# Perceiver block on one Trainium2 core: VectorE's fills, mask and layer-norm variances placed elsewhere in the query stage

## What is computed

```
x = x + _L0_xattn_ref(_layernorm(x, axis=-1), ctx_1024, _lenS2, Wq, Wk, Wv, Wo, q_norm_w, k_norm_w)
    # _layernorm: m = mean(x); v = var(x); (x - m) / sqrt(v + 1e-05)
    # _L0_xattn_ref: qh = rms_norm((q @ Wq) per head, q_norm_w); kh = rms_norm((kv @ Wk) per head, k_norm_w)
    #                mask = arange(s) < x_seqlens;  attn = softmax(where(mask, qh kh^T / 8, -1e9));  o = (attn vh) @ Wo
x = x + _L0_attn_ref(_layernorm(x), ...)
x = x + _L0_ffn_ref(_layernorm(x), ...)
```

## Time and profile before

| | us |
|---|---|
| median of 3 runs | 2426.11 |
| lowest, highest | 2424.57, 2427.75 |
| the profiled execution | 2425.77 |
| its span in the trace | 2423.9 |
| PE busy | 2319.3 (96%) |
| DVE busy | 2101.4 (87%) |
| ACT busy | 1363.6 (56%) |
| POOL busy | 1485.0 (61%) |

### The profile page before, as it was taken

One profiled execution on the slowest core, in us unless ns is written; L12 is line 12 of the kernel. 1 busy time (PEld: TensorE's weight loads), 2 busy tenths in 40 slices (PEclk: granted clock), 3 DMA queues, 4 the chain that ended last, 5 costly groups with the idle time before them and its releaser, 6 DMA issues. The chain is left out here.

```text
span 2423.9 us, 57393 instructions
## 1 busy us (share of the span) xinstructions
PE 2319.3 (96%) x16343; PEld 1961.3 (81%) x16343; DVE 2101.4 (87%) x3379; ACT 1363.6 (56%) x2591; POOL 1485.0 (61%) x1069
## 2 busy tenths in 40 slices
PE   6888999999999999999999999999999999899985
PEld 3666888888888888888888888888888888788743
DVE  6779999999999999999999999999999997558776
ACT  4744555555555555555555555555555554355646
POOL 3446777777777777777777777777777772001100
PEclk9999999999999999999999999999999999999987
DMA  2432222222222222222222222222222214331000
GB/s 92 158 125 48 47 56 54 54 54 54 54 54 54 54 54 54 54 53 53 53 54 54 55 59 55 54 53 53 53 53 53 53 46 136 124 106 37 2 1 18
DMA packets 441099, 145.04 MB, mean 60 GB/s; under 512 B 365344, under 2 KB 423616, under 8 KB 440896
## 3 DMA queue, kind: packets, MB, share of 16 engines
q1 hardware_dynamic: 440880, 143.50, 23.9%
q10 hardware_dynamic: 144, 0.52, 0.1%
HBM read 109.17 MB, written 34.73 MB: 59 GB/s over the span
## 5 line engine op out<-in xcount | busy, mean ns | idle before, releaser
L456 POOL TENSOR_TENSOR probs<-arena,best_all 128x1024 f32 (+2 forms) x397 | 943.2, 2376 | 422.0 <-DVE best L835 401.3
L1079 PEld LDWEIGHTS u_ps<-rows,probs 128*128 128x128 f32 x6656 | 801.3, 192 | 56.7 <-issue 13.7
L1079 PE MATMUL u_ps<-rows,probs 128*128 (+1 forms) x6656 | 812.5, 276 | 9.8 <-ACT probs L661 5.0
L820 DVE SCALAR_TENSOR_TENSOR arena<-s_ps,mask,rrms 128x512 f32 (+2 forms) x832 | 603.6, 727 | 113.4 <-PE s_ps L956 112.2
L661 ACT ACTIVATE probs<-probs 128x1024 f32<-128x1024 f32 (+1 forms) x416 | 440.9, 1061 | 418.9 <-POOL probs L456 404.1
L795 DVE TENSOR_REDUCE ssq<-squares 128x16 f32<-128x1024 f32 (+2 forms) x416 | 490.3, 1179 | 37.2 <-ACT squares L619 36.0
L619 ACT ACTIVATE squares<-k_ps 128x512 f32<-128x512 f32 (+1 forms) x832 | 450.6, 590 | 41.6 <-PE k_ps L956 21.9
L835 DVE TENSOR_TENSOR best<-best,arena 128x1024 f32<-128x1024 f32 (+1 forms) x352 | 448.3, 1274 | 0.1
L954 PE MATMUL k_ps<-w_hi,cT_hi 128*128 128x512 f32 (+1 forms) x832 | 362.4, 436 | 4.4 <-ACT squares L619 4.4
L613 ACT ACTIVATE cT_hi<-cT 128x128 fp32r<-128x128 f32 (+1 forms) x416 | 129.2, 311 | 365.5 <-DVE cT L786 365.4
L954 PE MATMUL s_ps<-q_hi,cT_hi 128*128 (+2 forms) x832 | 330.4, 397 | 3.1 <-DVE arena L820 3.0
(11 more groups left out here) (245 smaller groups left out, 2209.7 us busy)
## 6 DMA issues: line engine op xcount, KB each, us to landing
stage<-in_ctx SPq DMA_DIRECT2D x1536, 16.0 KB, 1.7
rows<-in_ctx SPq DMA_DIRECT2D x32, 768.0 KB
queries<-probs SPq DMA_DIRECT2D x16, 1024.0 KB, 4.0
q_plain<-queries SPq DMA_DIRECT2D x32, 512.0 KB, 3.4
best_all<-best_rows SPq DMA_DIRECT2D x31, 512.0 KB, 3.7
u_transposed<-uT_sb SPq DMA_DIRECT2D x124, 128.0 KB, 2.6
a_uT<-u_transposed SPq DMA_DIRECT2D x10, 1024.0 KB, 4.9
arena<-u_transposed SPq DMA_DIRECT2D x6, 1024.0 KB, 4.9
```

The lines of the kernel that those rows point to most:

```text
L456: pool.tensor_tensor(probs[0:r, slot_of(c, PRING), :], scores_at(b, c), best_all[0:r, bass.ds((b % 2) * HL, HL)], ALU.subtract).then_inc(s ...
L820: dve.scalar_tensor_tensor(out=scores_at(p, c, h * HALF, HALF).rearrange("p (h l) -> p h l", l=L), in0=s_ps[h][0:r, :].rearrange("p (h l) ...
L1079: last = pe.matmul(u_ps[g // 3][:, at:at + UW], probs[0:r, s, g * P:(g + 1) * P], rows, start=(c == 0 and g % 3 == 0), stop=(c == NC - 1), ...
```

## The change

DVE's list is written in another order, and `layernorm_variance` is cut into four parts (mean; centred rows; squares; variance), each with its own waits on one semaphore, `ln_var`, which now counts six for a chunk. The work itself is the same, instruction for instruction.

- The 26 fills and the fill of `ssq` stand in front of everything on DVE, ahead of `layernorm_variance(0)`.
- `make_mask` and `layernorm_variance(1)` stand behind `layernorm_scale(0)`, ahead of step 0.
- `w_lo` stands in step 2 instead of step 0.
- The four parts of `layernorm_variance(2)` stand at the ends of steps 0 to 3, those of `layernorm_variance(3)` at the ends of steps 4 to 7, each ahead of the step's `layernorm_scale` and `turn`.

```diff
@@ ACT: rough_layernorm(j)
-                act.wait_ge(ln_var, 2 * j + 2)
+                act.wait_ge(ln_var, 6 * j + 6)
@@ DVE: layernorm_variance
-            def layernorm_variance(j):
+            def layernorm_variance(j, quarter):
...
+                if quarter == 0:
+                    dve.wait_ge(x_in[j], 16)
+                    dve.tensor_reduce(stat[:, 0, :], x3, AX_X, ALU.add).then_inc(ln_var, 1)
+                    dve.wait_ge(ln_var, 6 * j + 1)
+                    dve.tensor_scalar(stat[:, 1, :], stat[:, 0, :], 1.0 / D, None, ALU.mult).then_inc(ln_var, 1)
+                elif quarter == 1:
+                    dve.wait_ge(ln_var, 6 * j + 2)
+                    dve.tensor_tensor(xn3, x3, bc(stat[:, 1, :], [P, CHUNK, D]), ALU.subtract).then_inc(ln_var, 1)
+                elif quarter == 2:
+                    dve.wait_ge(ln_var, 6 * j + 3)
+                    dve.tensor_tensor(xsq3, xn3, xn3, ALU.mult).then_inc(ln_var, 1)
+                else:
+                    dve.wait_ge(ln_var, 6 * j + 4)
+                    dve.tensor_reduce(stat[:, 2, :], xsq3, AX_X, ALU.add).then_inc(ln_var, 1)
+                    dve.wait_ge(ln_var, 6 * j + 5)
+                    dve.tensor_scalar(stat[:, 3, :], stat[:, 2, :], 1.0 / D, EPS, ALU.mult, ALU.add).then_inc(ln_var, 1)
@@ DVE: query(i)
-                if i == 0:
-                    for j in range(2 * NC):
-                        dve.memset(rows1[:, j * UW + D:j * UW + D + 1], 1.0).then_inc(ones_ready, 1)
-                    dve.memset(ssq[:, :], 0.0).then_inc(ssq_clear, 1)
-                    dve.wait_ge(ssq_clear, 1)
-                    make_mask()
-                    layernorm_variance(1)
+                if i == 2:
                     dve.wait_ge(w_hi_ready, 1)
                     dve.tensor_tensor(w_lo[:, :], u_sb[:, :], w_hi[:, :], ALU.subtract).then_inc(w_ready, 1)
-                if i % CHUNK == 0 and CHUNK <= i < TILES - CHUNK:
-                    layernorm_variance(i // CHUNK + 1)
+                if i + 2 * CHUNK < TILES:
+                    layernorm_variance(i // CHUNK + 2, i % CHUNK)
                 if i % CHUNK == 1 and i + 3 < TILES:
                     layernorm_scale((i + 3) // CHUNK)
@@ DVE: ahead of the steps
-            layernorm_variance(0)
+            for j in range(2 * NC):
+                dve.memset(rows1[:, j * UW + D:j * UW + D + 1], 1.0).then_inc(ones_ready, 1)
+            dve.memset(ssq[:, :], 0.0).then_inc(ssq_clear, 1)
+            dve.wait_ge(ssq_clear, 1)
+            for quarter in range(4):
+                layernorm_variance(0, quarter)
...
             layernorm_scale(0)
+            make_mask()
+            for quarter in range(4):
+                layernorm_variance(1, quarter)
             each_step(dve, query, step)
```

More of the change, by code:

```diff
@@ L719, in layernorm_scale @@
                 dve.wait_ge(ln_rough, j + 1)
-                newton(dve, stat[:, 3, :], stat[:, 4, :], stat[:, 5, :], stat[:, 0, :], ln_steps, 7 * j + 4)
-                dve.wait_ge(ln_steps, 7 * j + 7)
+                newton(dve, stat[:, 3, :], stat[:, 4, :], stat[:, 5, :], stat[:, 0, :], ln_steps, 3 * j)
+                dve.wait_ge(ln_steps, 3 * j + 3)
                 dve.tensor_tensor(xn3, xn3, bc(stat[:, 0, :], [P, CHUNK, D]), ALU.mult).then_inc(xn_ready, 1)
```

## The result

| | before, us | after, us |
|---|---|---|
| median | 2426.74 (4 runs) | 2411.67 (4 runs) |
| lowest, highest | 2424.57, 2427.75 | 2408.80, 2413.31 |
| the profiled execution, its span | 2425.77, 2423.9 | 2413.20, 2411.4 |

The ratio is 0.9938, with a 95% interval of 0.9921 to 0.9955: 15.1 us between the medians, and 12.6 us between the two profiled executions. Predicted was 2410.6, 1.1 us under the median, in a range from 2406 to 2418.5.

A forecast was written before the change was run, and what follows sets the result against it. PE's some 33 us idle in the query stage, behind ACT's waits for DVE's variances, was taken as the bound; 6.8 + 3.2 + 6.8 - 1.3 = 15.5 us off the median 2426.11 gave 2410.6 us, range 2406 to 2418.5.

The forecast's parts named there:

- Fills: Fills at DVE's front, before x lands at 3.94: cost 0, allowed 0 to 0.3 us.
- Mask and `layernorm_variance(1)` in the gap: In DVE's idle time before save_q(0): done by 14.5, PE delivers at 14.69, 0.2 us to spare; 0 to 0.5 allowed.
- Term A: Steps 0 to 3: ACT's 4.71 us wait goes and save_q comes earlier; gain 6.8 us, between 5.5 and 7.3.
- that chain keeps its lengths: Steps 1 to 3: POOL's L475 still starts 2.94 us after save_q and ends 1.90 later, setting the next save_q.
- the first rival, clock: PE stays at 1.2 GHz longer in tiles 2 and 3: gain 12, 2414 us; chance 0.20 shared with DVE-bound steps.
- Term B: Step 4: one whole variance leaves, the step falls from 9.10 to 5.91 us; gain 3.2, between 2.3 and 3.2.
- Term C: Steps 8 and 9: the other variance leaves, 13.1 us instead of 19.93; gain 6.8, or 5.9 if steps cost 7.0.
- Term D: Steps 5 to 7: the variance parts cost time as DVE and POOL block each other; -1.3 us, between 0 and -3.8.
- The sum: All four terms together: 6.8 + 3.2 + 6.8 - 1.3 = 15.5 us gained.
- Everything behind it is the same length.: After the query stage: later passes keep their length, so the stage's gain of about 15.5 us comes out whole.

The follow-up runs named there:

- sp_later: The changed kernel with SP's context loads one query step later, so query stores stand ahead of them: 2411.77 us, ratio 0.9941.
- wlo_3: The changed kernel with w_lo in step 3 instead of step 2: 2408.29 us, ratio 0.9927.
- before_again: The kernel before the change, unchanged, run for a second trace: 2428.41 us (one run).
- after_again: The changed kernel, unchanged, run again beside its variants: 2411.98 us, ratio 0.9952.
- wlo_1: The changed kernel with w_lo in step 1 instead of step 2: 2410.02 us, ratio 0.9934.
- parts_only: The changed kernel with fills, mask, layernorm_variance(1) and w_lo back behind save_q(0), variances still in parts: 2417.45 us, ratio 0.9967.
- best: The changed kernel with w_lo in step 1, SP's context loads one step later and filler matmuls in PE's idle time: 2410.26 us, ratio 0.9932.
- early_w: The changed kernel with w_hi ahead of step 0, w_lo in DVE's front gap, mask in step 17, SP's loads one step later: 2410.85 us, ratio 0.9953.

## Why the prediction was right, point by point

**What bounds the kernel.** Right for the stage: PE's busy time there stayed, its idle time went. That what is won comes out whole at the end is not what the profiled execution shows: 13.5 us at the last save, 12.5 at the end, with 8.7 in the passes between.

**Fills.** 0, as predicted: 1.84 to 2.85, with 1.26 us to spare before x lands.

**Mask and `layernorm_variance(1)` in the gap.** Right, but the 0.2 us to spare were 0: the lengths landed 0.3 us later (10.24 instead of 9.95), and the end is a dead heat at 14.6.

**Term A, predicted 6.8.** It is 6.13 us at full clock (`sp_later`, 38.44 - 32.31) and 4.88 in after. `save_q` of steps 1 to 3 was put at 17.45, 22.3 and 27.15 and stands at 17.34, 22.47 and 27.77. The step that failed is "that chain keeps its lengths". POOL's small instruction behind `save_q(2)` took 0.75 us instead of 0.21, since DVE's `w_lo` and squares stand there. POOL's timeline of after:

```profile
24.20 0.75 POOL L463 TENSOR_TENSOR arena<-arena 128x16 f32<-128x16 f32 x1 [1.68 <-ACT arena L560]
...
25.92 1.90 POOL L475 TENSOR_TENSOR arena<-arena 128x1024 f32<-128x1024 f32 x1
```

L475 ends at 27.82 instead of 27.2, and both PE's turn and DVE's L734 wait for it: 0.6 of the 0.7 us. `wlo_3` bears this out: with `w_lo` gone from there the small one takes 0.22 us, and PE's turn starts at 27.48 instead of 28.01 in `sp_later`. The other 1.25 us in after are the first rival, clock: it was set against a sentence that "no gap over 2 us is left there", and one of 2.54 us is left. It cost 1.3 us and not 3.7, because only the turn and one half ran slow.

**Term B, 3.2.** 9.10 less 5.91 is 3.19. That it is exact is in part luck of the trace: in `before_again` the same step takes 10.26 us, as PE runs at half clock behind the 3.11 us of idle time, and the term is 4.35.

**Term C, 6.8.** 19.93 less 14.12 is 5.8 in after, and 19.93 less 13.14 is 6.8 in `sp_later`. The wait for the store (0.68 us, and 0.2 in the next step) is most of the difference. The prediction spoke of SP only for the context loads; a shorter step brings the need for a buffer forward, and where SP's loads are issued slowly the store behind them doesn't move with it. The 6.8 us also hold something that the prediction did not see. In before, `save_q(9)` starts as PE's L974 ends, and that took 2.05 us at half clock instead of 1.12. By an estimate from these two numbers, 0.9 of the 6.8 us are the clock, which came back because the 3.64 us of idle time went.

**Term D, -1.3.** Steps 5 to 8 take 18.10 us against 17.74: -0.36. The price of the lock was mis-sized because DVE came first. DVE and POOL in step 5 of after:

```profile
42.38 0.69 DVE L726 TENSOR_TENSOR arena<-arena 128x512 f32<-128x512 f32 x1
...
44.24 0.93 DVE L734 TENSOR_SCALAR arena<-arena 128x16 f32<-128x16 f32 x1
```

```profile
42.61 0.54 POOL L469 TENSOR_TENSOR arena<-arena 128x16 f32<-128x16 f32 x1
43.23 1.90 POOL L475 TENSOR_TENSOR arena<-arena 128x1024 f32<-128x1024 f32 x1
```

L726 runs in 0.69 us, where the price was taken from one that took 2.39, and POOL's small one is stretched instead, to 0.54. The Trainium skill (SBUF — State Buffer, section SBUF: two separate sides) has whoever starts first hold the shared ports for the whole instruction; these rows agree, on both sides: 0.93 us for 0.17 on DVE, 0.54 for 0.22 on POOL.

**The sum, 15.5.** At full clock and without the store's wait it is 6.13 + 3.19 - 0.36 + 6.79 = 15.8 us (`sp_later`). In after's trace it is 4.88 + 3.19 - 0.36 + 5.81 = 13.5. Both are against the first trace of before; against the second, after's gain at the last save is 15.9. So the stage gives 13.5 to 15.9 us, and the forecast of 15.5 is right in its mechanism. That the median's 15.1 us comes within 0.4 of it is partly luck: in the profiled execution the stage gave 2 us less than the sum, 4.8 were lost behind it (4.3 of them in the two places shown), and 3.8 won at the end. Other executions have other sums, and no trace shows that of the median. The other 0.6 of the 1.1 us by which the forecast was off is before's own median, 2426.74 us here and 2426.11 when the sum was made.

**"Everything behind it is the same length."** Wrong in the profiled execution by 4.8 us one way and 3.8 the other. A gain as in the clock rival (12) is what it had, 12.6, though of the places that the rival named only the turn and half of step 4 ran slow.

**The clock rival's evidence.** It was set against the reading that after the 3.11 us of the earlier trace rows PE "ran on at full rate". That holds for the one trace; in `before_again` it did not, and in before itself it did not behind the 3.64 us of step 9.

## What to carry to other kernels

Work that stands behind a wait of another engine can be moved into idle time ahead of it, and the gain can be read step by step from the spacing of one repeated instruction; add for each moved two-input DVE instruction what the large and also the small POOL instructions beside it do, and for each shortened step which buffer is needed earlier and what its store is queued behind. Where a gain of some 15 us is to be refined by 1 us, compare traces at a marker inside the stage, since the time of the whole carries the clock of all later stages. Take such a marker from two traces of the same kernel before a single difference is believed. And when a wait is removed, look whether PE ran slow behind it: part of the gain may be its clock.

## What the runs showed of the hardware

**The clock after short idle times is not the same from one execution to the next.** Behind the same 2.54 us of PE idle time the turn ran in 1.94 us in both traces of after and in 1.06 in `sp_later`. Behind the 2.2 us ahead of the first product with the values, the 16 matmuls took 2.02 us in both traces of before, in `after_again` and in `wlo_1`, and 2.93 to 3.67 us in the other seven traces without fillers. In `wlo_1` it fell behind 1.40 us of idle time, in after (126.25) behind 0.88, and in `parts_only` behind 0.79: the group of 16 at 123.82 took 1.90 us for 1.16. The Trainium skill (TensorE: Matmul & The Clock Gate, section HAM oscillation — how this bites in real kernels) puts the fall of the clock down to long idle gaps between groups of matmuls; in these traces it also fell at gaps of 0.79 to 2.54 us, so short ones aren't safe. What decides it in an execution was not settled.

**The mean clock goes with the spread.** The runs of one kernel lie 1.3 us (`best`) to 8.7 us (`early_w`) apart, and the slowest have a lower mean granted clock than the fastest: 2406.39 us at 0.991 and 2413.85 at 0.988 for `wlo_1`. By an estimate from these, a mean of 0.001 less over 2410 us is 2.4 us of work at full clock. That this clock causes the difference, and isn't caused by it, was not tested apart.

**A column of 16 is enough to be stopped.** DVE's L734, 128x16 with one input, takes 0.17 us where it comes before POOL's L475 (25.15 in `wlo_3`) and 1.81 behind it (26.04 in after). DVE's 128x1024 sum, L731, wasn't lengthened: it ran from 19.79 to 21.00 in after, in its usual 1.21 us, across the start of POOL's L475 at 20.62.
